# FFN stage: scaling and sums of the attention weights behind the two halves of the gated rows, in place of between them

## The chip, the cores and the metric

One Trainium2 chip, one of its cores in use. Times are microseconds of device time for one execution of the program. The kernel before takes 1093.36 us (median of 3 runs, 1090.88 to 1095.32). The metric is that time.

## The reference

The reference layer-normalises `x` (4 batches of 512 tokens, 512 features), and computes two branches from the normalised rows `xn`:

```
xn  = layernorm(x)
q,k,v = xn @ W_Q/W_K/W_V + bias           # 16 heads of 128
s   = softmax(causal(q @ k^T / sqrt(128))) @ v, then @ W_O + b_O
g   = (xn @ gate_w^T) * gate_s ; u = (xn @ up_w^T) * up_s      # 1408 hidden features
f   = silu(((silu(g) * u) @ down_w^T) * down_s)
out = x + s * f
```

Everything is float32 outside. The kernel multiplies in float16: each float32 operand is split into two float16 halves, the rounded value and what is left ("hi" and "lo"), and a product is two or three passes over the halves.

## The kernel before, in words

The engines' programs are written out by hand: each engine runs its list strictly in order, and semaphores (`wait_ge`, `then_inc`) tie the lists together. Nothing reorders them. The work has two stages: the FFN (first 250 us) and the attention (the rest).

**The FFN stage** runs over four chunks c = 0 to 3 of 512 tokens, and within each over m = 0 to 10, the 11 blocks of 128 hidden features. A step is written c.m below (2.5 is chunk 2, block 5). In a step TensorE (`step` in the tensor block) does three things, each 8 matmuls of 512 columns: the gate product of m into the bank `GATE`, the up product of m into the bank `UP`, and the down product of m-1. Before gate(m) it waits for `gate_silu` of m-1 (the bank is read), before up(m) for `hidden_ok` of m-1, before down(m-1) for `ht_lo` of m-1.

ScalarE in a step: silu of the gate bank (L1154, `gate_silu`), then what is passed as `amid`, then the float16 half of the gated rows (L1158, `ht_hi`), which waits for `hidden_ok`. VectorE in a step: the product silu(g) * u (L1493, `hidden_ok`), then what is passed as `amid`, then the second half of the gated rows (L1498, `ht_lo`), which waits for `ht_hi`. In steps c.0 both also scale and park the output of the chunk before (L1485, L1145).

**Beside the steps of chunks 1 to 3 the attention weights are prepared.** Ten steps per chunk (m = 1 to 10) hold one slot each, numbered 0 to 28: slot = 10 (c-1) + m-1. A slot of a set of 16 may have:
- two scalings on ScalarE (`scale_weights`, L1099: `w_in` times 16, in place), in 14 of the 29 slots, so 28 instructions: slots 0, 1, 5, 6, 10, 11, 14, 15 and the same again from 16. They wait for the load of `w_in`.
- one or two sums on VectorE (`sum_weights`, L1403: differences of `w_in` tiles), 23 instructions in slots 1 to 4, 6 to 9, 11 to 13 and again from 17 on
- one or two splits: the hi half on ScalarE (`split_weights`, L1115), then the lo half on VectorE (L1387). In slots 4, 9, 12, 13, 20, 25 and 28 the last hi half waits for a sum of the same slot.
- a store of the halves, issued on ScalarE's DMA queue in the middle of the next step (L1170), and a load of the next `w_in` tiles from SyncE's queue (L463).

**Also beside the steps:** the rows of the next chunk are normalised (L1414 to L1432 on VectorE, L608 and L614 on GpSimd), combined (L1472 to L1478), and split into halves (L1140 ScalarE, L1460 VectorE). Then SyncE turns them with DMA transposes into `XT` or `ST` (L458): it waits for the ScalarE halves, issues the first transpose, issues the loads of x (L431), waits for the VectorE halves, and issues the second. Its `w_in` loads stand behind these in its list. Row splits stand in steps c.1 and c.2 (to `ST`), c.6 and c.7 (to `XT`, chunks 1 and 2) and 3.7 and 3.8 (to `ST`, read by the first attention products). In steps 1.6 and 2.6 the row split on ScalarE waits for VectorE's normalised rows, which VectorE computes behind its lo halves of the slot.

Of the kernel before, what the change touches and what calls it, by code (L numbers as in the profile page):

```python
# [42 lines left out]
MT = F // P  # L43
# [13 lines left out]
FFN_SLOTS = 29  # L57
# [54 lines left out]
def build(nc, x, ffn_w, attn_w, cols, b_o, down_s, out):  # L112
# [10 lines left out]
    with ExitStack() as ctx:  # L123
# [256 lines left out]
        def nth_split(g, j, e):  # L380
            return SPLITS * g + 7 * j + e
# [18 lines left out]
        def split_to(g, j, e):  # L400

            if j < 2:
                return qk_w[g * HG:(g + 1) * HG, :, e, j, :].rearrange("h p n -> p h n")
            return v_w[g, :, V_ORDER.index(e)] if j == 2 else o_w[g, :, e]

        def split_from(g, j, e):
            rows = W_OUT[OUT_OF[nth_split(g, j, e)]]
            return rows.rearrange("p (h n) -> p h n", h=HG) if j < 2 else rows
# [669 lines left out]
        def _(act):  # L1078
# [14 lines left out]
            def scale_weights(slot):  # L1093

                g, i = divmod(slot, SLOTS)
                j, _ = SLOT_SPLITS[i]
                for b in SLOT_SCALES.get(i, ()):
                    act.wait_ge(w_loaded[b], 16 * (4 * g + j + 1))
                    nc.scalar.activation(w_in[:, b], w_in[:, b], ACT.Copy, scale=WS).then_inc(w_scaled, 1)  # L1099
# [25 lines left out]
            def split_rows(j, tiles):  # L1125

                if j > 0 and tiles[0] == (2 if j == 2 * (B - 1) else 0):
                    act.wait_ge(rows_turned, ROW_TURNS * j)
                for t in tiles:
                    if j % 2 == 0 and j < 2 * (B - 1):  # L1130
                        c = j // 2 + 1
                        if c == 1:
                            act.wait_ge(xn_ok, TT + t + 1)
                        elif t < 2:
                            act.wait_ge(xn_ok, 2 * (c + 2) + t + 1)
                        else:
                            act.wait_ge(xn_pool_ok, 2 * (c - 2) + t - 1)
                    else:
                        act.wait_ge(s_ok, 4 * ((j + 1) // 2) - (2 if t >= 2 and j == 2 * (B - 1) else 0))
                    nc.scalar.activation(XS[0][:, t], x_in[:, t], ACT.Copy).then_inc(xs_hi, 1)  # L1140

            def silu_down(c, tiles):
                for t in tiles:
                    act.wait_ge(down_scaled, TT * c + t + 1)
                    nc.scalar.activation(ffn_out[:, t], ffn_out[:, t], ACT.Silu).then_inc(down_silu, 1)  # L1145

            def park(c):
                act.wait_ge(down_silu, TT * (c + 1))
                act.dma_start(parked_chunks[c], ffn_out).then_inc(park_done, 16)

            def step(c, m, slot, down_of=None, amid=None):
                n = MT * c + m
                act.wait_ge(gate_mm, n + 1)
                nc.scalar.activation(silu_gate, GATE[:], ACT.Silu, scale=ffn_scales[:, ds(m, 1)]).then_inc(gate_silu, 1)  # L1154
                if amid is not None:
                    amid()
                act.wait_ge(hidden_ok, n + 1)
                nc.scalar.activation(HT[0][:, slot], hidden, ACT.Copy).then_inc(ht_hi, 1)  # L1158
                if down_of is not None:
                    silu_down(down_of, range(TT))  # L1160
                    park(down_of)

            def store_weights(slot):

                g, i = divmod(slot, SLOTS)
                j, splits = SLOT_SPLITS[i]
                for e in splits:
                    n = nth_split(g, j, e)
                    act.wait_ge(w_lo, n + 1)
                    act.dma_start(split_to(g, j, e), split_from(g, j, e)).then_inc(w_stored[OUT_OF[n]], 16)  # L1170

            def later_step(c, m):

                done = (MT - 1) * (c - 1) + max(m, 1) - 2
                stores = m != 1 and 0 <= done < FFN_SLOTS
                slot = (MT - 1) * (c - 1) + m - 1

                def weights():
                    if stores:
                        store_weights(done)  # L1180
                    if m > 0 and slot < FFN_SLOTS:
                        scale_weights(slot)

                step(c, m, 2 if m == MT - 1 else m % 2, down_of=c - 1 if m == 0 else None, amid=weights)
                if m == 7 and c < B - 1:
                    split_rows(2 * c, (2, 3))
                if m > 0 and slot < FFN_SLOTS:
                    split_weights(slot)
                if m in (1, 2):
                    split_rows(2 * c - 1, (0, 1) if m == 1 else (2, 3))  # L1190
                if m == 6 and c < B - 1:
                    split_rows(2 * c, (0, 1))
                if m in (7, 8) and c == B - 1:
                    split_rows(2 * c, (2, 3) if m == 7 else (0, 1))
# [26 lines left out]
            for c in range(1, B):  # L1221
                for m in range(MT):
                    later_step(c, m)
# [130 lines left out]
            for u in range(NU - 1):  # L1354
                slot = UNIT_SLOTS + u
# [10 lines left out]
        def _(dve):  # L1366
# [23 lines left out]
            def sum_weights(slot):  # L1390

                g, i = divmod(slot, SLOTS)
                j, _ = SLOT_SPLITS[i]
                for nth in SLOT_SUMS.get(i, ()):
                    to, a, b = ((0, 1, 0), (1, 3, 1), (3, 3, 0), (2, 2, 3))[nth]
                    if nth == 0:
                        dve.wait_ge(w_lo, nth_split(g, j, 0) + 1)
                        dve.wait_ge(w_scaled, 4 * (4 * g + j) + 2)
                    elif nth == 1:
                        dve.wait_ge(w_scaled, 4 * (4 * g + j) + 4)  # L1400
                    else:
                        dve.wait_ge(w_sum, SUMS * g + 4 * j + (1 if nth == 2 else 3))
                    nc.vector.tensor_tensor(w_in[:, to], w_in[:, a], w_in[:, b], ALU.subtract).then_inc(w_sum, 1)  # L1403
# [83 lines left out]
            def step(c, m, slot, down_of=None, amid=None):  # L1487
                n = MT * c + m
                if n > 0:
                    dve.wait_ge(ht_lo, n)  # L1490
                dve.wait_ge(gate_silu, n + 1)
                dve.wait_ge(up_mm, n + 1)
                nc.vector.scalar_tensor_tensor(out=hidden, in0=UP[:], scalar=ffn_scales[:, ds(MT + m, 1)],  # L1493
                                               in1=silu_gate, op0=ALU.mult, op1=ALU.mult).then_inc(hidden_ok, 1)
                if amid is not None:
                    amid()
                dve.wait_ge(ht_hi, n + 1)
                nc.vector.tensor_tensor(HT[1][:, slot], hidden, HT[0][:, slot], ALU.subtract).then_inc(ht_lo, 1)  # L1498
                if down_of is not None:
                    scale_down(down_of, range(TT))  # L1500

            def later_step(c, m):

                slot = (MT - 1) * (c - 1) + m - 1
                weighed = m > 0 and slot < FFN_SLOTS
                step(c, m, 2 if m == MT - 1 else m % 2, down_of=c - 1 if m == 0 else None,
                     amid=(lambda: sum_weights(slot)) if weighed else None)
                if m == 7 and c < B - 1:
                    split_rows(2 * c, (2, 3))
                if weighed:  # L1510
                    split_weights(slot)
                if m in (1, 2):
                    split_rows(2 * c - 1, (0, 1) if m == 1 else (2, 3))
                if c < B - 1:
                    if m in (4, 5):
                        token_stats(c + 1, (0, 1) if m == 4 else (2, 3))
                    if m == 5:
                        variances(c + 1)
                    if m == 6:
                        scale_x(c + 1, (0, 1))  # L1520
                        split_rows(2 * c, (0, 1))
                    if m in (9, 10):
                        combine_rows(c, m == 10)
                else:
                    if m == 4:
                        scale_x(c + 1, (0, 1))
                    if m in (5, 6):
                        combine_rows(c, m == 6)
                    if m in (7, 8):
                        split_rows(2 * c, (2, 3) if m == 7 else (0, 1))  # L1530
# [275 lines left out]
```

## Time and profile before

| | us |
|---|---|
| median of 3 runs (lowest, highest) | 1093.36 (1090.88, 1095.32) |
| the profiled execution | 1091.22 |
| its span in the profile | 1089.4 |
| TensorE busy in the span | 1064.1 |
| VectorE busy | 809.1 |
| ScalarE busy | 736.3 |
| GpSimd busy | 196.7 |

The span runs from the first to the last instruction that the profiler saw; the execution's own time holds 1.8 us more around it. Busy times are shares of one engine's time and run beside each other. The profile's page groups instructions by line, and its timelines list them in order of time: start, duration, engine, line, operation, and in brackets the idle time before it with what ended it. Where several instructions of one line follow each other closely they are merged (x2).

### The profile page before, as it was taken

The numbers are of one execution on the slowest core, as the hardware profiler recorded it, in microseconds if no ns is written. First come the engines' busy times: TensorE is split into PE (matmuls) and PEld (weight loads), VectorE is DVE, ScalarE is ACT, GpSimd is POOL, SyncE is SP. The second block draws the span as 40 slices with busy tenths as digits, with TensorE's granted clock in tenths as the row PEclk, the third lists the DMA queues.
The fourth block names the chain that finished last, engine by engine and source line by source line (L and its number), as shares of the span: only waits on it lengthen the run. The fifth ranks groups of instructions, "written<-read, shape, count | busy, mean of one in ns | idle before, by whom it ended". The sixth has DMA issues, their size and how long they took to land.

```text
span 1089.4 us, 21557 instructions
## 1 busy us (share of the span) xinstructions
PE 1064.1 (98%) x7452; PEld 706.2 (65%) x7452; DVE 809.1 (74%) x2005; ACT 736.3 (68%) x1832; POOL 196.7 (18%) x195
## 2 busy tenths in 40 slices
PE   6999999999999999999999999999999999999998
PEld 3444443446667777777777777777777777777764
DVE  7777876686777777777777777777777777776876
ACT  6856566556677776767777776777766666666662
POOL 1000202012101121122312212232000001144434
PEclk9999999999999999999999999999999999999999
DMA  7436676687777769878886897879667667868866
GB/s 270 147 77 184 146 206 188 167 254 202 161 206 208 180 168 261 181 182 213 222 232 168 212 233 161 219 176 263 162 132 199 142 144 180 230 167 233 215 163 172
DMA packets 318533, 207.67 MB, mean 191 GB/s; under 512 B 251872, under 2 KB 284640, under 8 KB 317920
## 3 DMA queue, kind: packets, MB, share of 16 engines
q1 hardware_dynamic: 295872, 179.64, 67.0%
q10 hardware_dynamic: 19200, 15.73, 4.5%
q0 software_dynamic: 3360, 11.01, 2.7%
q8 instruction: 56, 0.92, 0.3%
q14 instruction: 45, 0.37, 0.1%
HBM read 109.87 MB, written 34.60 MB: 133 GB/s over the span
## 4 chain that ended last, share of the span: by engine, by line
PE 86%; ACT 6%; DVE 4%; issue 1%; SPq 1%; DMA 1%; ACTq 0%; DVEq 0%
PE bank L731 77%; PE bank L913 9%; ACT arena L1279 1%; DVE arena L1371 1%; SPq L458 1%; ACT arena L1293 1%; DMA w_in<-attn_w_dram 0%; PE bank L742 0%; DMA arena<-x_dram 0%; DVE bank L1646 0%; DVE arena L1493 0%; SPq L431 0%; ACT Q L1246 0%; DVE arena L1593 0%; ACT arena L1158 0%
## 5 line engine op out<-in xcount | busy, mean ns | idle before, releaser
L731 PE MATMUL bank<-XT,arena 128*128 128x256 f16 (+2 forms) x1872 | 310.6, 314 | 2.3 <-ACT arena L1154 2.1
L731 PE MATMUL bank<-arena 128*128 128x512 f16 (+1 forms) x1124 | 269.2, 379 | 0.8 <-DVE arena L1498 0.6
L731 PEld LDWEIGHTS bank<-XT,arena 128*128 128x128 f16 (+1 forms) x1872 | 179.8, 98 | 110.6 <-issue 4.6
L1279 ACT ACTIVATE arena<-bank,neg_max 128x512 f32<-128x512 f32 (+3 forms) x256 | 132.8, 525 | 138.8 <-DVE neg_max L1646 138.8
L731 PE MATMUL bank<-ST,arena 128*128 128x256 f16 x1536 | 199.4, 273 | 1.3 <-DVE arena L1588 0.5
L731 PEld LDWEIGHTS bank<-arena 128*128 128x128 f16 x1124 | 109.6, 98 | 108.2 <-issue 1.5
L731 PEld LDWEIGHTS bank<-ST,arena 128*128 128x128 f16 x1536 | 148.0, 98 | 25.7 <-ACT arena L1236 3.4
L1663 DVE SCALAR_TENSOR_TENSOR arena<-arena,inv_sum 128x512 f16<-128x512 f32 (+3 forms) x256 | 127.2, 559 | 9.6 <-ACT arena L1293 7.3
L1646 DVE CUSTOM_DVE_ANT_0 bank<-bank,mask 128x512 f32<-128x512 f32 (+3 forms) x256 | 118.0, 517 | 21.5 <-PE bank L731 21.3
L1293 ACT ACTIVATE arena<-arena,inv_sum 128x512 f16<-128x512 f32 (+3 forms) x256 | 122.4, 557 | 0.0
L731 PE MATMUL bank<-K,Q 128*128 128x512 f16 (+3 forms) x768 | 114.7, 299 | 3.0 <-ACT K L1250 2.5
L913 PE MATMUL bank<-arena,V 128*128 128x512 f16 x756 | 113.0, 299 | 1.5 <-issue 0.9
L731 PEld LDWEIGHTS bank<-K,Q 128*128 128x128 f16 x768 | 66.3, 98 | 54.8 <-issue 6.6
L913 PEld LDWEIGHTS bank<-arena,V 128*128 128x128 f16 x756 | 68.0, 98 | 40.9 <-issue 3.0
L731 PE MATMUL bank<-arena,ST 128*128 128x256 f16 x576 | 78.4, 273 | 0.8 <-ACT arena L1279 0.4
L1246 ACT ACTIVATE Q<-arena 128x256 f16<-128x256 f32 x64 | 26.6, 416 | 69.0 <-DVE arena L1593 69.0
L635 POOL TENSOR_TENSOR w_out<-w_in,w_out 128x512 f16<-128x512 f32 x28 | 33.0, 1189 | 163.0 <-DVE K L1609 163.0
L1588 DVE TENSOR_TENSOR arena<-bank,arena 128x256 f32<-128x256 f32 x64 | 27.2, 424 | 46.3 <-PE bank L731 46.3
L731 PEld LDWEIGHTS bank<-arena,ST 128*128 128x128 f16 x576 | 56.0, 98 | 8.0 <-ACT arena L1279 0.7
L1158 ACT ACTIVATE arena<-arena 128x512 f16<-128x512 f32 x44 | 27.5, 625 | 44.0 <-DVE arena L1493 43.8
L1493 DVE SCALAR_TENSOR_TENSOR arena<-bank,ffn_scales,arena 128x512 f32<-128x512 f32 x44 | 32.9, 747 | 31.3 <-PE bank L731 25.6
L731 PE MATMUL bank<-arena,XT 128*128 128x256 f16 x384 | 52.0, 273 | 0.0
(124 smaller groups left out, 1447.4 us busy)
## 6 DMA issues: line engine op xcount, KB each, us to landing
arena<-split_qk SPq DMA_DIRECT2D x64, 896.0 KB, 5.3
w_in<-attn_w_dram SPq DMA_DIRECT2D x64, 256.0 KB, 4.3
arena<-ffn_w_dram SPq DMA_DIRECT2D x8, 768.0 KB, 4.7
arena<-x_dram SPq DMA_DIRECT2D x20, 256.0 KB, 4.1
parked_silu<-arena ACTq DMA_DIRECT2D x4, 1024.0 KB, 4.5
arena<-split_o SPq DMA_DIRECT2D x4, 1024.0 KB, 6.9
split_qk<-w_out ACTq DMA_DIRECT2D x15, 256.0 KB, 4.1
split_qk<-w_out SPq DMA_DIRECT2D x13, 256.0 KB, 3.6
```

Of the source, the lines that this page charges most:

```text
L458: sp.dma_start_transpose(out=to[part][:, c].rearrange("p t k q -> p (t k) q"), in_=XS[part].rearrange("p t d -> p (t d)")).then_inc(rows_t ...
L635: nc.gpsimd.tensor_tensor(split_rows_out(g, j, e, 1), split_rows_in(j, e), split_rows_out(g, j, e, 0), ALU.subtract).then_inc(w_lo, 1)
L731: mm = nc.tensor.matmul(out, stationary(a, k), moving(b, k), start=first and n == 0 and i == 0, stop=last and n == len(tiles) - 1 and i == ...
L913: return nc.tensor.matmul(ZB[:, j * P:], V[a][:, (u // HG) % 2, j, ds((u % HG) * E, E)], PT[b][:, (J_STEP + 1) * j:J_STEP * j + TT, :].rea ...
L1158: nc.scalar.activation(HT[0][:, slot], hidden, ACT.Copy).then_inc(ht_hi, 1)
L1246: nc.scalar.activation(halves(Q[0], 1), sums[:, 1], ACT.Copy).then_inc(q_hi, 1)
L1279: e = nc.scalar.activation(probs[:, at:at + width], SC[b_][:, col:col + width], ACT.Exp, bias=neg_max[:, i:i + 1], scale=-1.0, accum_out=r ...
L1293: nc.scalar.activation(query_blocks(0, i), probs_by_block(i, at), ACT.Copy, scale=inv_sum[:, i:i + 1]).then_inc(p_hi, 1)
L1493: nc.vector.scalar_tensor_tensor(out=hidden, in0=UP[:], scalar=ffn_scales[:, ds(MT + m, 1)], in1=silu_gate, op0=ALU.mult, op1=ALU.mult).th ...
L1588: nc.vector.tensor_tensor(sums[:, 2], halves(QB, 0), sums[:, 2], ALU.add).then_inc(sum_ok, 1)
L1646: nc.vector.tensor_tensor_reduce(out=SC[b_][:, col:col + width], in0=SC[b_][:, col:col + width], in1=mask[:, S - width:], scale=-SCORE_SCA ...
L1663: nc.vector.scalar_tensor_tensor(out=query_blocks(1, i), in0=probs_by_block(i, at), scalar=inv_sum[:, i:i + 1], in1=query_blocks(0, i), op ...
```

## The change

On ScalarE `scale_weights(slot)` no longer runs inside `step` between silu and the half of the gated rows; it is called after `step`, ahead of the row split of m = 7 and of `split_weights(slot)`. The store of the slot before stays in the middle. On VectorE `sum_weights(slot)` no longer runs between the gated product and its lo half, but after `step`, ahead of the row split of m = 7 and of the lo halves of the weights. No instruction is added or dropped, and no semaphore or count changes.

```diff
@@ scalar block, later_step @@
-                def weights():
-                    if stores:
-                        store_weights(done)
-                    if m > 0 and slot < FFN_SLOTS:
-                        scale_weights(slot)
-
-                step(c, m, 2 if m == MT - 1 else m % 2, down_of=c - 1 if m == 0 else None, amid=weights)
+                step(c, m, 2 if m == MT - 1 else m % 2, down_of=c - 1 if m == 0 else None,
+                     amid=(lambda: store_weights(done)) if stores else None)
+                if m > 0 and slot < FFN_SLOTS:
+                    scale_weights(slot)
                 if m == 7 and c < B - 1:
                     split_rows(2 * c, (2, 3))
                 if m > 0 and slot < FFN_SLOTS:
@@ vector block, later_step @@
                 weighed = m > 0 and slot < FFN_SLOTS
-                step(c, m, 2 if m == MT - 1 else m % 2, down_of=c - 1 if m == 0 else None,
-                     amid=(lambda: sum_weights(slot)) if weighed else None)
+                step(c, m, 2 if m == MT - 1 else m % 2, down_of=c - 1 if m == 0 else None)
+                if weighed:
+                    sum_weights(slot)
                 if m == 7 and c < B - 1:
                     split_rows(2 * c, (2, 3))
                 if weighed:
```

## Rows read from the trace of the kernel before

**Rows 1.** The page's first part: busy time, share of the span, instructions.
```profile
PE 1064.1 (98%) x7452; PEld 706.2 (65%) x7452; DVE 809.1 (74%) x2005; ACT 736.3 (68%) x1832; POOL 196.7 (18%) x195
```

**Rows 2.** Waits, 60 to 260 us: engine, line, releaser: total, times, longest.
```profile
ACT arena L1158 <- DVE arena L1493: 42.4, 28, 2.3
...
PE bank L731 <- ACT arena L1154: 2.1, 1, 2.1
```

**Rows 3.** Groups by line, 60 to 260 us: count, busy, mean ns, idle before.
```profile
L1099 ACT ACTIVATE w_in<-w_in 128x512 f32<-128x512 f32 x28 | 16.1, 621 | 7.0 <-DMA w_in<-attn_w_dram 4.1 <-issue 1.4 <-DVE Q L1387 0.8
L1403 DVE TENSOR_TENSOR w_in<-w_in 128x512 f32<-128x512 f32 x23 | 15.5, 682 | 0.0
...
L1115 ACT ACTIVATE w_out<-w_in 128x512 f16<-128x512 f32 x22 | 13.3, 614 | 0.0
```

**Rows 4.** The chain of waits in order of time: start, duration, what.
```profile
143.10 0.90 ACT w_in L1099 x2
...
150.66 3.24 SPq L458
...
161.84 4.44 DMA w_in<-attn_w_dram
...
177.59 82.29 PE bank L731 x416
```

**Rows 5.** Timeline of ScalarE, steps 2.1 and 2.2.
```profile
143.00 1.14 ACT L1099 ACTIVATE w_in<-w_in 128x512 f32<-128x512 f32 x2
...
146.69 1.14 ACT L1099 ACTIVATE w_in<-w_in 128x512 f32<-128x512 f32 x2
...
149.50 1.13 ACT L1140 ACTIVATE V<-arena 128x512 f16<-128x512 f32 x2
```

**Rows 6.** Timeline of TensorE: gate(1.8), gate(2.2), gate(2.6), down(2.5), gate(2.8).
```profile
117.48 3.62 PE L731 MATMUL bank<-XT,arena 128*128 x16
...
143.38 3.62 PE L731 MATMUL bank<-XT,arena 128*128 x16
...
164.10 3.62 PE L731 MATMUL bank<-XT,arena 128*128 x16
168.34 1.90 PE L731 MATMUL bank<-arena 128*128 x8 [0.62 <-DVE arena L1498]
...
177.59 3.62 PE L731 MATMUL bank<-XT,arena 128*128 x16 [2.08 <-ACT arena L1154]
```

**Rows 7.** Timelines of ScalarE and VectorE, steps 2.5 to 2.7.
```profile
165.22 0.63 ACT L1099 ACTIVATE w_in<-w_in 128x512 f32<-128x512 f32 x1 [3.68 <-DMA w_in<-attn_w_dram]
...
170.99 0.75 DVE L1493 SCALAR_TENSOR_TENSOR arena<-bank,ffn_scales,arena 128x512 f32<-128x512 f32 x1
...
176.78 0.67 ACT L1154 ACTIVATE arena<-bank,ffn_scales 128x512 f32<-128x512 f32 x1
```

**Rows 8.** The same timelines, steps 1.6 and 1.7.
```profile
110.88 0.75 DVE L1493 SCALAR_TENSOR_TENSOR arena<-bank,ffn_scales,arena 128x512 f32<-128x512 f32 x1 [0.15 <-PE bank L731]
...
112.93 0.69 DVE L1387 TENSOR_TENSOR K<-w_in,K 128x512 f16<-128x512 f32 x1
...
116.06 0.67 ACT L1154 ACTIVATE arena<-bank,ffn_scales 128x512 f32<-128x512 f32 x1
```

**Rows 9.** The same timelines, steps 2.0 and 2.1.
```profile
136.78 0.75 DVE L1493 SCALAR_TENSOR_TENSOR arena<-bank,ffn_scales,arena 128x512 f32<-128x512 f32 x1 [0.51 <-PE bank L731]
...
142.42 0.69 ACT L1154 ACTIVATE arena<-bank,ffn_scales 128x512 f32<-128x512 f32 x1 [0.44 <-ACT arena L1145]
```

**Rows 10.** Timeline of all engines, step 3.8 to the first attention products.
```profile
240.69 1.13 ACT L1140 ACTIVATE V<-arena 128x512 f16<-128x512 f32 x2
...
241.85 6.34 SPq L458 DMA_TRANSPOSE ST<-V  x2
...
252.24 1.25 PEld L731 LDWEIGHTS bank<-ST,arena 128*128 128x128 f16 x12 [0.28 <-DMA ST<-V]
```

**Rows 11.** Stretches: busy time (instructions) by engine, then clock and DMA.
```profile
174.00:178.00 4.00, 1.92 (x9) 0.70 (x8) 3.82 (x9) 2.38 (x5) 3.09 (x2) 1.00 0.62 207
```

## The prediction

> **What bounds the kernel now.** I read the page's busy shares first, then the waits and the groups by line of the stretch in which the change lies (60 to 260 us), then the chain of waits, and last the timelines around each idle gap of TensorE. The shares say TensorE: busy 98% of the span, with ScalarE at 68% and VectorE at 74% [rows 1]. In the FFN stage the reader should see a rhythm: gate(2.2) starts at 143.38 and gate(2.6) at 164.10, so a step is (164.10 - 143.38) / 4 = 5.18 us with no gap; 117.48 + 5 x 5.18 = 143.38 says the same of chunk 1 [rows 6]. TensorE stands still twice: 0.62 us before down(2.5), and 2.08 us before gate(2.8), for the silu of step 2.7 [rows 2, 6]. The chain of waits shows what the shares hide. From before 143 until 177.59 it is not on TensorE at all: it goes over two scalings of step 2.1 (0.90 us, L1099), SyncE's transpose at 150.66, the `w_in` load that lands at 166.28, then VectorE and ScalarE to the silu of 2.7; from 177.59 on it is TensorE for 82 us [rows 4]. So the stage is bound by TensorE, except in this one stretch, where anything added to the chain comes out at the end.
>
> **What a moved scaling costs.** The 28 scalings take 621 ns each [rows 3], but follow each other every 0.52 us: a pair that takes 1.14 us [rows 5] holds ScalarE for 1.04. In the old place ScalarE mostly stood idle: the half of the gated rows waited for VectorE's product 28 times, 42.4 us in all [rows 2], up to 2 us a step. Behind the half, the pair is no longer beside that wait but in front of the splits of the slot. Nothing new is computed; each of the 14 pairs can put up to 1.04 us on what follows it in its step: the hi halves of weights and rows, and by them VectorE's lo halves, SyncE's transposes and loads, and the next silu. TensorE needs silu(m) by the start of gate(m+1). A third of the step is gate(m), so 5.18 x 2/3 = 3.45 us are left for a silu of 0.69 us [rows 9], 2.6 us of slack after the hand-overs: in most steps the cost is nothing. The 23 sums (682 ns, L1403 [rows 3]) had their idle place too; moved, they hold VectorE about 0.6 us behind the lo half, where it mostly has slack, and in slots 4, 9, 12, 13, 20, 25 and 28 ScalarE's last hi half now waits for them. What can be won: `ht_lo` no longer stands behind a scaling that waits for its load. Four places matter.
>
> *Step 1.6 (slot 5).* Slot 4 in step 1.5 first: with VectorE's lo half starting at t, its sum ran before t, and the second weight lo half started at t + 1.2. Now the sum runs from t + 0.61 to t + 1.29, ScalarE's hi half to t + 1.95 (614 ns, L1115 [rows 3]), and the lo half starts at t + 1.97: 0.76 later. VectorE had 0.15 us idle before the product of 1.6 at 110.88 [rows 8], and 0.1 more in small gaps; 0.53 stays. From that product to the weight's lo half were 112.93 - 110.88 = 2.05 us. Now: product 0.75, hi half 0.53, scalings 1.04, split 0.61 and four hand-overs 0.07, 3.00 us, so 0.95 later. Both sum to 1.48. The lo half is followed by the normalised rows, the row split and the silu of 1.7: it goes from 116.06 to 117.54 and ends at 118.21; TensorE starts 0.14 behind it, at 118.35, where 117.48 was due [rows 6, 8]. **+0.87 us.** Bounds 0 (the 0.75 us of slack between 116.73 and 117.48 covers all) and 1.5.
>
> *Step 2.0.* Slot 9 has the same late sum: +0.76 on VectorE, less its idle 0.51 before the product of 2.0 at 136.78 [rows 9], leaves 0.25. That goes over the down product's scaling to the silu of 2.1 at 142.42, which ends at 143.11, with 143.38 due and 0.14 needed: **+0.12 us.** Bounds 0 and 0.3.
>
> *The chain of steps 2.1 to 2.7.* In 2.1 and 2.2 ScalarE works without a pause, so both pairs come out: the row split that ended at 150.63 [rows 5] ends 1.04 + 0.86 (0.18 us of the second stood beside other waiting) + 0.13 later, **2.03**. SyncE's first transpose starts right on it, at 150.66 [rows 4], and its list (transpose, loads of x, transpose, `w_in`) runs without a pause, so the scaling of 2.5 that began at 165.22, when its load landed [rows 7], goes to 167.25. There the change gives back: the gated half is done before it, and `ht_lo` is no longer late, so the 0.62 us before down(2.5) go; and the splits follow the second scaling directly, 0.6 us sooner on VectorE. The silu of 2.6 ends at 170.55, gate(2.7) starts at 170.7 instead of 170.07. The product of 2.6 goes from 170.99 [rows 7] to 172.40 (+2.03 - 0.62 = +1.41), and the scalings of slot 15 add 0.95 as in step 1.6: silu of 2.7 from 176.78 to 179.14, gate(2.8) from 177.59 to 179.95. **+2.36 us.** Bounds: if SyncE's list absorbs all of the 2.03, the load lands as before and 0.95 - 0.62 = +0.33 is left; if nothing is given back, 2.03 + 0.95 = +3.0. I take 2.36, since the chain shows no slack on SyncE between 150.66 and 161.84 [rows 4].
>
> *Steps 3.8 to attention.* The row split of 3.8 started at 240.69 behind the weight splits; the pair of slot 27 now stands before it, +1.04 (in the old place it stood beside the wait for the product). SyncE's transposes at 241.85 follow it directly, and TensorE's weight load at 252.24 waited 0.28 us for just these rows [rows 10]: TensorE lost no time by it yet, but the slack is next to nothing. I leave 0.1 us of it: **+0.9 us.** Bounds 0 (transposes absorbed in the DMA queue) and 1.1.
>
> All other steps keep their time by my reckoning, but thinly: silu(2.3) has 0.3 us left, silu(1.8) and (2.8) 0.5, silu(3.2) 0.2 (its store's long issue included).
>
> Sum: 0.87 + 0.12 + 2.36 + 0.9 = **+4.3 us**, between +0.3 and +5.9 by the bounds. Against the profiled execution's own 1091.22 us that is 1095.5; the median of the three runs is 2.1 us above that execution, so I forecast 1093.36 + 4.3 = 1097.7.
>
> The Trainium skill, Perfetto Trace Analysis, "Identifying the Most-Contended Engine", takes the engine with the highest occupancy as the one to look at, and for ScalarE and VectorE occupancy as a fair measure. By it a reorder on engines at 68% and 74% would cost nothing and the time would stay 1093.4. The chain's 34 us without TensorE is what this case's trace sets against it.
>
> **The rivals.**
> 1. *The cover holds*: slack that I don't see (SyncE's list shortens when it starts later, the row split is not what the silu waits for) leaves at most +1 us: 1093.4 to 1094.4. For it: most steps have 2 us of idle ScalarE. Against it: the chain names the moved instructions.
> 2. *The other side, not slower*: the two stalls come from the scaling of 2.5, which held back `ht_hi`, `ht_lo` and then all of 2.6. With the halves first, 0.79 us (gate(2.7) at 170.07 for a due 169.28) and 2.08 us go: 1093.4 - 2.9 = 1090.5. It decides where the load lands no later than now and the splits of 2.6 start no later. Against it: those splits stand behind the scalings now, and the load behind two more.
> 3. *Thin margins break*: the margins of 0.2 to 0.5 us above are overrun one after the other, 0.5 us each over four or five, plus the sum at its upper bound: +6 to +8, 1099.4 to 1101.4. For it: five places within 0.5 us.
> 4. *The clock*: before gate(2.8) TensorE would now stand still about 3.5 us (down(2.6) starts with its `ht_lo` at about 174.7 and takes 1.73, to 176.4; gate(2.8) at 179.95). Through the 2.08 us of now the granted clock stayed at 1.00, the 2.4 GHz level [rows 11]; no row shows a longer gap in mid-kernel. Should it fall to 1.2 GHz for half a step to a whole one, 2.6 to 5.2 us come on top: +7 to +9.5, 1100.4 to 1102.9. The Trainium skill (TensorE: Matmul & The Clock Gate, "Why this matters for your kernels") warns of idle gaps between bursts for this reason; the row of 2.08 us neither bears it out nor denies it.
>
> **How the numbers follow.** Forecast 0.62, cover holds 0.15, not slower 0.05, thin margins 0.11, clock 0.07. A measurement of this kernel tells about 0.5% (5.5 us) from no change. Faster by that needs 1087.9 or less, which no case gives; 0.03 is for what I don't see. Slower by that needs 1098.8 or more: rivals 3 and 4, 0.18, and one in five of the forecast's cases with the runs' own spread of 2 us, 0.12: 0.30. The rest, 0.67, is within. Range: the bounds of the sum give 1093.7 to 1099.3; with the runs' spread, rival 1 and part of 2 to 4 it is 1091 to 1102.
>
> **What would show it.** Gate(2.8) starts some 3.35 us later than 177.59 (0.87 + 0.12 + 2.36), with an idle gap of 3 to 4 us before it; the gap of 0.62 before down(2.5) is gone, and a gap of about 1.4 stands before gate(2.7); a gap of 0.9 before gate(1.8); the transpose of 2.2 starts 2 us later against gate(2.2); the first product of `ST` waits about 1 us; from there on the attention stage is as long as before. The forecast is wrong if gate(2.8) starts less than 1.5 us or more than 5 us later, if steps of chunk 3 show new gaps, or if the granted clock leaves 1.00.

## The result, and the profile after

The changed kernel takes 1096.2 us (median of 19 runs, 1094.33 to 1099.17) against 1093.25 us of the kernel before (19 runs beside them): ratio 1.0027, 95% interval 1.0019 to 1.0035, so 2.95 us slower. The forecast was +4.3 us, 1097.7. The profiled execution took 1096.8 us, its span 1095.0, which is 5.6 us more than the span of before; where these 5.6 us lie is what the traces tell, and they are more than the medians' 2.95.

TensorE's timeline of the kernel after (start, duration, engine, line, operation; in brackets the idle time before and what ended it), the lines that answer to [rows 6] and the new gaps:

```profile
82.06 3.62 PE L731 MATMUL bank<-XT,arena 128*128 x16
...
119.24 3.62 PE L731 MATMUL bank<-XT,arena 128*128 x16 [0.75 <-ACT arena L1154]
...
145.19 3.62 PE L731 MATMUL bank<-XT,arena 128*128 x16
...
172.22 1.90 PE L731 MATMUL bank<-XT,arena 128*128 x8 [0.96 <-ACT arena L1154]
174.82 1.90 PE L731 MATMUL bank<-XT,arena 128*128 x8 [0.70 <-DVE arena L1490]
176.55 1.89 PE L731 MATMUL bank<-arena 128*128 x8
181.48 5.31 PE L731 MATMUL bank<-XT,arena 128*128 x16 [3.04 <-ACT arena L1154]
186.63 1.89 PE L731 MATMUL bank<-arena 128*128 x8
188.36 3.62 PE L731 MATMUL bank<-XT,arena 128*128 x16
```

Two lines of the kernel before that [rows 6] leaves out, gate(1.1) and gate(2.9), stand here for comparison:

```profile
81.22 3.62 PE L731 MATMUL bank<-XT,arena 128*128 x16
...
182.78 3.62 PE L731 MATMUL bank<-XT,arena 128*128 x16
```

The reader should take differences of the starts, place by place. (The idle time in brackets is some 0.17 us shorter than the delay: a group's duration reaches that far past the start of the next one even where nothing waits, as 186.63 + 1.89 = 188.52 for 188.36.) Gate(1.8) is at 119.24 for 117.48 [rows 6]: 1.76 us later, of which 0.84 was there by gate(1.1) (82.06 for 81.22, and no step before it is touched by the change), so +0.92. Gate(2.2) is 1.81 later: +0.05. Gate(2.8) is at 181.48 for 177.59, 3.89 later: **+2.08**. The gap before down(2.5) is gone; in its place gate(2.7) waits 0.96 us for the silu of 2.6 and up(2.7) 0.70 us for the product of 2.6, and 3.04 us stand before gate(2.8). Together with the differences before it, +0.92 + 0.05 + 2.08, the new order makes 3.05 us by the traces. The 16 matmuls of gate(2.8) and up(2.8) then take 5.31 us in place of 3.62, and gate(2.9) is at 188.36 for 182.78, 5.58 later: **+1.69** that no wait explains. From there to the end of the span (5.6) nothing is added.

The stretches of the same trace, columns as in [rows 11] (the figure behind POOL's busy time and count is the granted clock), and below them the same stretches of the kernel before:

```profile
178.00:182.00 4.00, 0.96 (x6) 0.29 (x4) 3.81 (x9) 1.84 (x3) 3.21 (x2) 1.00 0.65 209
182.00:190.00 8.00, 8.00 (x31) 3.29 (x30) 4.88 (x9) 5.99 (x11) 1.44 (x1) 0.79 0.60 132
```
```profile
178.00:182.00 4.00, 4.00 (x20) 1.84 (x19) 3.26 (x6) 3.26 (x7) 1.55 (x1) 1.00 0.30 85
182.00:190.00 8.00, 8.00 (x39) 3.64 (x38) 5.46 (x10) 4.65 (x9) 0.00 (x0) 1.00 0.89 182
```

In 182 to 190 us TensorE's clock was granted at 0.79 on average: behind the 3 us gap it ran at the lower level, 1.2 GHz, for part of the stretch. In the profiled execution of the kernel before it stayed at 1.00.

The timelines of ScalarE and SyncE, answering to [rows 4, 5, 7, 10]:

```profile
153.87 0.61 ACT L1140 ACTIVATE V<-arena 128x512 f16<-128x512 f32 x1
...
169.16 1.31 ACT L1099 ACTIVATE w_in<-w_in 128x512 f32<-128x512 f32 x2 [2.71 <-DMA w_in<-attn_w_dram]
...
180.68 0.67 ACT L1154 ACTIVATE arena<-bank,ffn_scales 128x512 f32<-128x512 f32 x1
```
```profile
154.51 2.98 SPq L458 DMA_TRANSPOSE ST<-V  x1
157.54 2.01 SPq L431 DMA_DIRECT2D arena<-x_dram  x4
159.59 4.34 SPq L458 DMA_TRANSPOSE ST<-V  x1
164.03 15.03 SPq L463 DMA_DIRECT2D w_in<-attn_w_dram  x8
...
248.47 4.79 SPq L458 DMA_TRANSPOSE ST<-V  x2
```

The first transpose of step 2.2 starts at 154.51 for 150.66 [rows 4]: 3.85 later, 2.04 of it since gate(2.2). The scaling of 2.5 starts 3.94 later, the silu of 2.7 3.90.

### The profile page after: what moved, and what is told of

It is laid out like the page before. It is cut to its first block, busy times and chain, and to the rows that moved or that the text cites. A ratio compares the mean times of both kernels' runs of the same rounds, so it can differ in the third digit from the quotient of the medians.

```text
span 1095.0 us, 21557 instructions
## 1 busy us (share of the span) xinstructions
PE 1066.8 (97%) x7452; PEld 706.6 (65%) x7452; DVE 810.0 (74%) x2005; ACT 736.1 (67%) x1832; POOL 197.2 (18%) x195
## 4 chain that ended last, share of the span: by engine, by line
PE 84%; ACT 6%; DVE 5%; issue 2%; SPq 1%; DMA 1%; POOL 0%; ACTq 0%; DVEq 0%
PE bank L731 75%; PE bank L913 9%; ACT arena L1276 1%; DMA b_o_rows<-b_o_dram 1%; SPq L458 1%; DVE arena L1368 1%; ACT arena L1290 1%; DVE arena L1490 1%; ACT w_in L1099 0%; DMA w_in<-attn_w_dram 0%; DVE bank L1644 0%; ACT V L1140 0%; DVE arena L1429 0%; ACT w_out L1115 0%; SPq L431 0%
## 5 line engine op out<-in xcount | busy, mean ns | idle before, releaser
L1495 DVE TENSOR_TENSOR arena<-arena 128x512 f16<-128x512 f32 x44 | 30.5, 693 | 33.9 <-ACT arena L1158 33.9
```

## The experiments

Twelve kernels. Each ratio is against the kernel before, run beside it.

**The kernel before again.** No edit.

> The kernel before once more, for a second trace of it and the clock of each of its runs. The question: the after trace is 5.6 us longer in its span than the before trace, the medians differ by 2.95 us. Theory A (the chain theory): the shown before trace is a lucky one, some 1 to 2 us under its median, because SyncE's transposes and the w_in landing vary from run to run; expect gate(2.8) later than 177.59 in this trace by 0 to 2 us, everything else the same, mean clock 1.000 in all runs. Rival: the two shown traces are typical and the medians differ for another reason; expect gate(2.8) at 177.6 within 0.3 and a span of 1089 to 1090. Ratio 1.000.

Measured: 1093.06 us (11 runs), ratio 0.9996 (0.9987 to 1.0005). Gate(2.8) at 178.07, 0.48 later than 177.59, 0.25 of it there already at gate(1.1) (81.47). Mean clock: 1.000 in 7 runs, 0.998 in 4. Its profiled execution (1093.95 us) was one of the four:

```profile
168.81 1.90 PE L731 MATMUL bank<-arena 128*128 x8 [0.85 <-DVE arena L1498]
...
178.07 5.31 PE L731 MATMUL bank<-XT,arena 128*128 x16 [2.08 <-ACT arena L1154]
```

So the clock also falls in the kernel before, behind its gap of 2.08 us, and then gate(2.8) and up(2.8) take the same 5.31 us. The theory's place for gate(2.8) (0 to 2 us later) held, but not its cause nor its clock of 1.000 in all runs; the rival missed with its span (1092.1 us for 1089 to 1090). The waits up to gate(2.8) vary by a quarter of a microsecond between the two traces, and the clock is what the shown pair of before and after mainly differed by. Over 98 runs of the kernel before (those beside the experiments, and this copy), 38 had a mean clock of 1.000 with a median of 1092.5 us, 4 had 0.999 with 1091.8, and 56 had 0.998 with 1094.0: the two large groups lie 1.5 us apart. (That an unprofiled run at 0.998 fell at this gap is inferred from the profiled ones.) The changed kernel had 9 runs at 1.000 (median 1095.0) and 10 at 0.998 (1096.9). Like with like, the change costs 2.5 us at the one and 2.9 at the other, and the share of falls is about the same (10 of 19, 56 of 98): the 1.69 us of the profiled pair belong to the clock, which falls in both kernels, and not to the change.

**Scalings only.** The edit is the ScalarE half of the diff; the sums stay in `amid`.

> The scalings moved, the sums left in their old place. Chain theory: nearly the whole cost. Gap of about 0.3 us before gate(1.8) (0.95 for the pair of slot 5, less 0.6 of slack), none at 2.0, the transpose of 2.2 starts 1.9 us later, gate(2.8) about 2 us later than in the kernel before, gap before it 3 us; ratio 1.0020 to 1.0027, a mean clock of 0.998 in about half of the runs. Rival (the sums carry half or more: late w_hi and loads): ratio under 1.0012.

Measured: 1096.22 us (11 runs), ratio 1.0023 (1.0012 to 1.0033), as forecast; 7 of the 11 runs had a mean clock below 0.999.

```profile
118.46 3.62 PE L731 MATMUL bank<-XT,arena 128*128 x16 [0.18 <-ACT arena L1154]
...
180.31 5.02 PE L731 MATMUL bank<-XT,arena 128*128 x16 [3.04 <-ACT arena L1154]
...
256.85 1.48 PE L731 MATMUL bank<-ST,arena 128*128 128x256 f16 x12 [0.28 <-DMA ST<-V]
```

**Sums only.** The VectorE half of the diff; the scalings stay in `amid`.

> The sums moved, the scalings left in their old place. Chain theory: 0 to +0.3 us, ratio 1.000 (within 0.0005); the product of 1.6 is 0.5 us later but silu(1.7) still in time, gap before gate(2.8) 2.1 us as before, mean clock 1.000 in all runs. Rival (the sums carry half or more): ratio 1.0013 or more.

Measured: 1094.32 us (11 runs), ratio 1.0007 (0.9998 to 1.0016): by its interval neither no change nor the rival's 1.0013 is excluded. The mean clock was forecast at 1.000 in all runs and was 0.998 in 8 of the 11, so the median is of runs with a fall (1094.4 us, against 1094.0 for the same runs of the kernel before beside them). The trace holds 1.45 us before down(2.5) in place of 0.85 (the load landed 0.45 us later than in the second trace of before) and nothing else new. The two halves together make the whole within their intervals, 0.0023 + 0.0007 against 0.0027, and the scalings are the larger part. The traces say the same: from gate(1.1) to gate(2.8) are 96.37 and 96.60 us in the two traces of before, 97.26 with the sums moved, 98.45 with the scalings moved, 99.42 with both. In step 1.6 they split otherwise: the gap before gate(1.8) is 0.18 us with the scalings alone and 0.75 with both, so there the sum of slot 4 makes 0.57 of it; with the sums alone no gap shows there.

**Four of the fourteen pairs.**

```diff
+                behind = slot in (5, 10, 11, 15)
                 def weights():
                     if stores:
                         store_weights(done)
-                    if m > 0 and slot < FFN_SLOTS:
+                    if m > 0 and slot < FFN_SLOTS and not behind:
                         scale_weights(slot)
                 step(c, m, ..., amid=weights)
+                if m > 0 and behind:
+                    scale_weights(slot)
```

> Only the pairs of scalings of slots 5, 10, 11 and 15 moved behind the gated half, the other ten pairs and all sums in their old place. Chain theory: the same time as with all fourteen pairs moved, within 0.0007 in the ratio (1.0018 to 1.0027), with the same gaps before gate(1.8) (0.3 us) and gate(2.8) (3 us, a little more since slot 14 still holds back the gated half: gate(2.7) then about 2 us later and down(2.5) waits 2.5 us). Rival (each moved pair costs a little, by the number of pairs): 4/14 of it, ratio under 1.001.

Measured: 1095.71 us (11 runs), ratio 1.0022 (1.0011 to 1.0034), for 1.0023 with all fourteen. Nine of the 11 runs had a mean clock of 0.998, against 7 of 11 below 0.999 there, so the times hold different shares of falls. The distance from gate(1.1) to gate(2.8) is free of that: 98.93 us (81.37 to 180.30) for 98.45 with all fourteen.

```profile
117.98 3.62 PE L731 MATMUL bank<-XT,arena 128*128 x16 [0.19 <-ACT arena L1154]
...
170.09 1.90 PE L731 MATMUL bank<-arena 128*128 x8 [1.86 <-DVE arena L1502]
...
180.30 3.62 PE L731 MATMUL bank<-XT,arena 128*128 x16 [3.04 <-ACT arena L1154]
```

The cost is that of places, not of the number of pairs: the ten others add nothing. Before down(2.5), 2.5 us were expected and 1.86 stand there.

**The kernel before, loads early.**

```diff
 def turn_rows(...):        # SyncE; for step 2.2 it is now given slot 12
     ...
             load_x(load)
+            if between is not None:
+                weight_traffic(between)      # the w_in loads of slot 12, left out at their old place
     sp.dma_start_transpose(...)              # the second transpose
```

> The kernel before, with one change in SyncE's list: the two w_in loads of slot 12 stand before the second transpose of the rows of step 2.2 instead of behind it. Chain theory (both gaps of the kernel before come from the load that lands late behind the transposes): no wait of the scalings in step 2.5, no gap before down(2.5) and gate(2.8), gate(2.8) 2.9 us earlier against the start of chunk 1, and with no gap in mid-stage the mean clock is 1.000 in every run; about 1089.5 us, ratio 0.9966 (0.9958 to 0.9975). Rival (the row split of step 2.6 waits for VectorE whatever the load does): only the 0.85 us before down(2.5) go and 2 us stay before gate(2.8), ratio 0.999.

The loads of slot 12 bring the tiles that slot 14 scales in step 2.5, those of slot 13 the tiles that slot 15 scales in step 2.6.

Measured: 1090.52 us (5 runs), ratio 0.9964 (0.9951 to 0.9977). The gap before down(2.5) is gone, one of 1.42 us is left before gate(2.8):

```profile
176.33 3.62 PE L733 MATMUL bank<-XT,arena 128*128 x16 [1.42 <-ACT arena L1156]
```
```profile
169.48 1.15 ACT L1101 ACTIVATE w_in<-w_in 128x512 f32<-128x512 f32 x2 [2.48 <-DMA w_in<-attn_w_dram]
```

The scalings of step 2.6 now wait 2.48 us for the loads of slot 13, which still stand behind the transpose: they are issued from 163.76 on and land at 169.4. So my account of one late load was half of it: with the first moved, the next takes its place. No run had a mean clock below 0.999, and that is part of the 0.0036: by the distance from gate(1.1) to gate(2.8), 94.82 us, the edit is worth 1.6 to 1.8 us, and the medians differ by 2.8.

**The changed kernel, loads early.** The same edit on the kernel after.

> The changed kernel with the same change in SyncE's list. Chain theory: the 2 us that the pairs of steps 2.1 and 2.2 put on the transposes no longer reach anybody; left are the pairs that stand in front of the splits in steps 1.6 and 2.6: a gap of 0.75 us before gate(1.8) and 0.8 to 1 us before gate(2.8), nothing before gate(2.7) or down(2.6); ratio to the kernel before 0.998 to 0.999 (1.7 us above the kernel before with early loads), mean clock 1.000 in most runs since no gap is as long as 2 us. Rival (it is the moved pairs as such that cost 3 us): ratio above 1.0000.

Measured: 1093.71 us (11 runs), ratio 1.0002 (0.9993 to 1.0011). A miss: 0.8 to 1 us were expected before gate(2.8), 2.80 stand there, and the ratio, forecast at 0.998 to 0.999, is where the rival put it or just below.

```profile
178.33 5.31 PE L733 MATMUL bank<-XT,arena 128*128 x16 [2.80 <-ACT arena L1156]
```
```profile
167.13 0.69 DVE L1386 TENSOR_TENSOR w_out<-w_in,w_out 128x512 f16<-128x512 f32 x1 [0.87 <-ACT w_out L1117]
...
170.04 0.75 DVE L1492 SCALAR_TENSOR_TENSOR arena<-bank,ffn_scales,arena 128x512 f32<-128x512 f32 x1
```

The load no longer waits, but the pair of slot 14 (step 2.5) holds VectorE back 0.87 us before its lo halves, and the row statistics behind them bring the product of 2.6 to 170.04, 1.6 us after TensorE had finished up(2.6) (gate(2.6) at 165.01, and 3.45 for gate and up); the pair of slot 15 then adds its own, 0.62 us of it waiting for the late loads of slot 13. I had reckoned this place as a copy of step 1.6, where step 1.5 has no scalings. What follows: early loads take 0.0025 off the changed kernel's ratio too, but it stays 3.2 us above the kernel before with the same loads. By the traces 2.35 us of that are waits (97.17 us from gate(1.1) to gate(2.8) for 94.82); the rest fits the clock, which fell in 6 of 11 runs here and in none of 5 there. The chain over SyncE is one road by which the moved pairs reach the end, the direct one over VectorE is another, and it is nearly as long.

**The changed kernel, loads early, rows first.** VectorE's normalised rows of steps 1.6 and 2.6 before the lo halves of the weights:

```diff
+                if m == 6 and c < B - 1:
+                    scale_x(c + 1, (0, 1))
                 if weighed:
                     split_weights(slot)
...
                     if m == 6:
-                        scale_x(c + 1, (0, 1))
                         split_rows(2 * c, (0, 1))
```

> The changed kernel with early loads, and in steps 1.6 and 2.6 VectorE normalises the rows before the lo halves of the weights instead of behind them. Chain theory: no gap is left in the FFN stage, the same time as the kernel before with early loads within 0.0007 (ratio to the kernel before about 0.9966): the new order then costs nothing and brings nothing. Rival (the moved pairs still cost by thin margins): new gaps of 0.3 us or more, ratio above 0.9978.

Measured: 1089.78 us (10 runs), ratio 0.997 (0.9958 to 0.9982). The only gap of the stage is a new one of 0.21 us before gate(2.9):

```profile
180.61 3.62 PE L733 MATMUL bank<-XT,arena 128*128 x16 [0.21 <-ACT arena L1156]
```

That is 0.0006 from the kernel before with early loads, inside the 0.0007 forecast, though "no gap" was out by these 0.21 us. With both ways to the silu of 2.7 shortened, no cost of the new order can be told within the intervals.

**The kernel before, rows first.** The same edit on the kernel before, loads as they were.

> The kernel before, loads as they were, with VectorE's normalised rows of steps 1.6 and 2.6 before the lo halves of the weights. Chain theory: the gap before down(2.5) stays at 0.6 to 0.9 us, the gap before gate(2.8) falls from 2.1 to about 0.9 us (two lo halves of 0.6 us leave the path); ratio 0.9985 by the gaps alone, 0.998 if the clock then stays at 1.000 in all runs. Rival: the row split waits for something else, gap unchanged.

Measured: 1091.02 us (10 runs), ratio 0.9977 (0.9967 to 0.9986), no run below a mean clock of 0.999; the gap before down(2.5) is 1.06 us, a little over the 0.6 to 0.9 expected.

```profile
168.55 1.90 PE L731 MATMUL bank<-arena 128*128 x8 [1.06 <-DVE arena L1498]
...
176.61 3.72 PE L731 MATMUL bank<-XT,arena 128*128 x16 [0.89 <-ACT arena L1154]
```

The gap falls from 2.08 to 0.89 us, two lo halves of 0.60, as forecast.

**The kernel before, loads early, rows first.** Both edits on the kernel before.

> The version that the runs so far point to: the kernel before (scalings and sums in their old place), the two loads of slot 12 before the second transpose of step 2.2, and VectorE's normalised rows of steps 1.6 and 2.6 before the lo halves of the weights. Early loads alone left a gap of 1.42 us before gate(2.8), rows first took 1.2 us off the same gap: 0.2 us left, no gap at down(2.5), mean clock 0.999 to 1.000 in all runs. Ratio to the kernel before 0.9955 (0.9945 to 0.9965), 1088.5 us, below both kernels and below early loads alone. Rival (the gain of early loads alone was mostly the clock, and is had only once): the same as early loads alone, 0.9964 or more.

Measured: 1089.64 us (11 runs), ratio 0.9967 (0.9956 to 0.9979). No gap of TensorE from 68 to 258 us; gate(2.8) at 175.21, 10.36 us after gate(2.6) at 164.85, two steps of 5.18. This version beats both kernels, by 4.2 us the one (1093.79, run beside it) and by some 6.5 the other (by the ratios, 0.9967 and 1.0027). Of the 4.2 us, 3.1 are waits (93.24 us from gate(1.1) to gate(2.8) for 96.37); the rest fits the clock, which no longer falls. The forecast of the ratio missed: 0.9967 lies outside 0.9945 to 0.9965 and is what the rival said, no better than the 0.9964 of early loads alone. In the traces it does save 1.6 us over early loads alone (93.24 for 94.82), and the times don't show it; that one rests on five runs, and the difference stays open.

**Slot 27 alone.** As with the four slots, with `behind = slot == 27`.

> The kernel before with only the pair of scalings of slot 27 (step 3.8) behind the gated half: the term of the forecast that did not show. Forecast's theory: transposes of 3.8 start 1.04 us later and the first ST product starts 0.9 us later. Rival, from the traces so far (four kernels with this pair moved issue the two transposes in 4.8 us, six with it in the old place in 6.3 to 6.5 us): the issue takes 4.8 us and the product starts within 0.3 us of its old distance from gate(3.8); ratio 1.000.

Measured: 1093.36 us (10 runs), ratio 1.0 (0.999 to 1.001).

```profile
244.71 4.83 SPq L458 DMA_TRANSPOSE ST<-V  x2
```
```profile
246.75 3.62 PE L731 MATMUL bank<-XT,arena 128*128 128x512 f16 x16
...
254.30 1.48 PE L731 MATMUL bank<-ST,arena 128*128 128x256 f16 x12
```

Gate(3.10) and the first `ST` product in the kernel before, then in the changed one:

```profile
244.94 3.62 PE L731 MATMUL bank<-XT,arena 128*128 128x512 f16 x16
...
252.29 1.47 PE L731 MATMUL bank<-ST,arena 128*128 128x256 f16 x12
```
```profile
250.52 3.62 PE L731 MATMUL bank<-XT,arena 128*128 128x512 f16 x16
...
257.87 1.47 PE L731 MATMUL bank<-ST,arena 128*128 128x256 f16 x12
```

From gate(3.10) to the first `ST` product are 254.30 - 246.75 = 7.55 us; in the kernel before 252.29 - 244.94 = 7.35, in the changed one 257.87 - 250.52 = 7.35. The issue takes 4.83 us for 6.34 [rows 10]: the rival's case, not the forecast's.

**A gap of 2 us, and of 5 us, by design.** On the version with early loads and rows first, ScalarE repeats one copy in step 2.6, three or eight times, each waiting for the one before:

```diff
+                if m == 6 and c == 2:
+                    ...
+                    for i in range(3):     # 8 in the other
+                        if i > 0:
+                            act.wait_ge(transposing, i)
+                        nc.scalar.activation(XS[0][:, 0], x_in[:, 0], ACT.Copy).then_inc(transposing, 1)
                 if m == 6 and c < B - 1:
                     split_rows(2 * c, (0, 1))
```

> The version with early loads and rows first, and in step 2.6 three more copies of a row tile on ScalarE (each waits for the one before; the same values into the same tile) ahead of the row split: one gap of TensorE of about 2.2 us before gate(2.8) and no other in mid-stage. Clock theory (a gap of 2 us lets the granted clock fall in a part of the runs, and a fall costs 1.5 to 1.9 us on top): +2.0 us in runs with mean clock 1.000, +3.6 us in runs with 0.998, both kinds among the runs. Rival (the fall has nothing to do with the gap): the same share of runs with 0.998 as without the gap.

> The same with eight copies: a gap of about 5.6 us before gate(2.8). Clock theory: the mean clock is below 1.000 in every run, and the time is above the version without a gap by the gap plus at least 1.5 us: +7 us or more (+5.4 without a fall). Rival (no tie between gap and clock): +5.4 us and some runs at 1.000.

Measured, three copies: 1092.14 us (12 runs), ratio 0.9992 (0.998 to 1.0004), the gap 1.76 us. Five runs at 1.000 (1091.3 to 1092.2), two at 0.999, four at 0.998 (1093.3 to 1095.1), one at 0.997 (1097.2): both kinds, as the clock theory has it. The medians at 1.000 and at 0.998 are 1091.7 and 1093.7, 2.1 and 4.1 us above the version without the gap (2.0 and 3.6 expected). Without the gap none of 11 runs was below 0.999. Eight copies: 1097.56 us (6 runs), ratio 1.0032 (1.002 to 1.0045), 7.9 us above the version without the gap, for a gap of 6.30 us: 1.6 us on top. All six runs are at 0.996 or 0.997.

```profile
182.78 5.00 PE L733 MATMUL bank<-XT,arena 128*128 x16 [6.30 <-ACT arena L1156]
```
```profile
178.00:182.00 4.00, 0.00 (x0) 0.00 (x0) 0.43 (x1) 3.84 (x8) 0.68 (x1) 0.60 0.40 141
182.00:186.00 4.00, 3.22 (x9) 1.23 (x10) 3.30 (x6) 3.75 (x8) 0.00 (x0) 0.55 0.31 109
186.00:190.00 4.00, 4.00 (x21) 1.77 (x19) 2.70 (x6) 2.99 (x5) 0.00 (x0) 1.00 0.97 196
```

The clock falls while TensorE stands still (0.60 in 178 to 182), stays low over its first matmuls (0.55), and is back in the third stretch. In the trace of the changed kernel, with 3.04 us, it was still 1.00 over the gap (178 to 182) and low only behind it.

## Why the prediction came out right, point by point

The direction, the size class and the places were right; the measured 2.95 us lie under the 4.3 by one term that was not there (+0.9 at step 3.8) and one that was a little large. Without step 3.8 the sum is 3.35 us, and the traces show 3.05.

*What bounds the kernel.* Right: the stage is TensorE's but for the stretch up to gate(2.8). Four pairs on named places (slots 5, 10, 11 and 15) cost as much as all fourteen, and the two edits that shorten the named chain make the kernel before 4.2 us faster.

*Step 1.6.* Forecast +0.87, measured +0.92 (the gap of 0.75 and the 0.17 above); that the sum of slot 4 matters as forecast shows in the 0.18 of scalings only.

*Step 2.0.* Forecast +0.12, measured +0.05.

*Steps 2.1 to 2.7.* Forecast +2.36, measured +2.08. The transposes moved by 2.04 for a forecast of 2.03, step 2.6's pair added what was worked out, and what was given back at 2.5 was larger by 0.3. One wait forecast at 1.4 us before gate(2.7) came as two, 0.96 there and 0.70 before up(2.7), and before gate(2.8) stand 3.04 us for about 3.5. What was given back is larger because the second load landed sooner behind the first than in [rows 7] (the pair of scalings took 1.31 us with its wait, in place of 1.71 from 165.22 to 166.93). But the belief that this is one chain, over SyncE, did not hold: with the loads early it cost nearly the same by way of VectorE.

*Step 3.8.* The term that failed, by "the slack is next to nothing", with +0.9 us. The forecast took the transposes' duration as fixed, and its own lower bound (absorbed) is what happened. Measured 0, and slot 27 alone 0.2 us in the trace and nothing in the time. The transposes do start later, but in the five traces with this pair moved they are issued in 4.76 to 4.83 us, in the nine with it in the old place in 6.33 to 6.53: the delay is given back. In the new order the first of ScalarE's two stores of slot 27 goes out 0.83 us before the first transpose (247.64 and 248.47), in the old one 0.16 us before it (241.69 and 241.85) and the second just behind it. That these stores are what slows the issue is likely, not shown: no kernel moved the stores alone.

*The thin margins* held: chunk 3 has no gap. *The clock* was a rival, and the forecast also named "the granted clock leaves 1.00" as a sign that it is wrong. That sign came. The clock does fall behind such a gap, in about half of the runs, for 1.5 to 2.1 us between the medians, mostly less than the rival's 2.6 to 5.2; but it did so in the kernel before as well, so it gave the change next to nothing, and the sign was a bad one. That the forecast's difference survived is partly luck: it never asked whether the kernel before fell too. The forecast's line that the clock stayed at 1.00 through 2.08 us [rows 11] was true of one execution and read as if of all.

## What to carry to other kernels

An engine at 68% can stand on the path that sets the end: before moving work on it, list the places where something with a deadline stands behind it in its own list, and count only those; here four of fourteen, and another (slot 14) once the loads came early. If a wait is hidden, work that fills it is free, and the same work behind the wait is not, whatever the busy share says. Where two ways of nearly equal length lead to one wait, shortening one shows only a part: in the changed kernel early loads alone took 0.0025 off the ratio, and both edits 0.0057; with both, the order in dispute no longer showed. And take a second trace of the kernel before, before explaining a difference of 0.2%.

## What the runs showed of the hardware

The granted clock fell behind an idle gap of TensorE of 1.76 to 3.04 us in a part of the runs of one and the same program, counting runs with a mean clock of 0.998 or less: 5 of 12 at 1.76, 56 of 98 in the kernel before at 2.08, 12 of 21 at 2.08 to 2.09 (sums only, and slot 27 alone), 6 of 11 at 2.80, 26 of 41 at 3.04 (10 of 19 in the changed kernel, 7 of 11 with scalings only, 9 of 11 with four pairs). It fell in all six runs at 6.30, in none of five at 1.42, and with no gap over 1.1 us in 1 of 31 runs. The share does not rise clearly between 1.76 and 3.04. A fall takes 1.4 to 1.7 us: the 16 matmuls behind the gap need 5.0 to 5.3 us in place of 3.62, once, and then the granted clock is back at 1.00, the 2.4 GHz level. The Trainium skill (TensorE: Matmul & The Clock Gate, "Why this matters for your kernels") warns of idle gaps of TensorE between bursts of matmuls. The runs agree that a gap brings the fall, but show it behind shorter gaps (1.76 and 2.08 us) than the page warns of.

Two DMA transposes of row tiles, one directly behind the other, held SyncE's list for 4.26 us (kernel before, at 67.16) to 6.61 us (scalings only, at 121.94). Nothing behind a transpose in the list goes out meanwhile: in the changed kernel the second one of step 2.2 takes 4.34 us from 159.59 on, and the `w_in` loads start at 164.03. What sets the length was not tested.
